# A hybrid layer kernel on one core: batch 0 prepared ahead of the turned weights, and one joint order for the setup and the first passes

## What is computed

```python
x = x + attention(_layernorm(x))    # w_qkv, b_qkv, w_out, b_out
x = x + ffn(_layernorm(x))          # router over 8 experts, top 2, and a shared expert
x = x + state_space(_layernorm(x))  # conv, scan over 512 tokens with 16 states
x = x + ffn(_layernorm(x))          # the same weights again
```

```python
q = jax.nn.elu(q) + 1
k = jax.nn.elu(k) + 1
rot_q = apply_rope(q)
rot_k = apply_rope(k)
attn_num = jnp.einsum('bhid,bhjd->bhij', rot_q, rot_k)
attn_denom = jnp.einsum('bhid,bhjd->bhij', q, k)
attn_weights = attn_num / attn_denom
```

## Time and profile before

| what | value |
|---|---|
| median of 3 runs | 3764.75 us (3763.28 to 3771.59) |
| profiled execution, its own time | 3763.91 us |
| its span, first to last instruction | 3761.8 us |
| PE busy | 3394.5 us (90%) |
| ACT busy | 3199.0 us (85%) |
| DVE busy | 2664.6 us (71%) |
| POOL busy | 1341.8 us (36%) |
| first score of pass 0 starts at | 73.94 us |
| `A.oT` of pass 0, 1 starts at | 168.25, 366.07 us |

### The profile page before, as it was taken

The page is one execution under the profiler, slowest core; times in us unless marked ns, Lnnn a source line. Parts: engine busy times, 40 slices in busy tenths (PEclk is TensorE's granted clock), DMA queues, the critical chain, the costliest instruction groups (busy, mean ns, idle before and its releaser), DMA issues. The chain is left out here.

```text
span 3761.8 us, 38380 instructions
## 1 busy us (share of the span) xinstructions
PE 3394.5 (90%) x11446; PEld 1446.9 (38%) x11446; DVE 2664.6 (71%) x3513; ACT 3199.0 (85%) x4034; POOL 1341.8 (36%) x758
## 2 busy tenths in 40 slices
PE   3896899999999999999999999999999999998847
PEld 1231334434343444434344443434344443434424
DVE  3537868687776868677686867778686877769582
ACT  2787899898999999899998989999998999886643
POOL 2112324344343434434342433424243443314251
PEclk9896899999999999999999999999999999999978
DMA  5324345455544545454454545454454645435332
GB/s 156 112 82 116 126 137 174 141 179 148 164 149 138 170 131 185 146 167 142 155 171 135 177 132 185 143 159 159 139 181 125 187 145 164 149 107 171 111 136 76
DMA packets 214847, 552.01 MB, mean 147 GB/s; under 512 B 25105, under 2 KB 96626, under 8 KB 214642
## 3 DMA queue, kind: packets, MB, share of 16 engines
q1 hardware_dynamic: 214642, 549.57, 47.4%
HBM read 488.65 MB, written 63.18 MB: 147 GB/s over the span
## 5 line engine op out<-in xcount | busy, mean ns | idle before, releaser
L785 PE MATMUL bank<-hF,wst 128*128 128x512 f32 x2304 | 1146.3, 619 | 29.7 <-ACT hF L887 15.2
L1332 POOL TENSOR_TENSOR yM<-yM,ws 128x1024 f32<-128x1024 f32 x240 | 630.6, 2628 | 1399.8 <-DVE ws L1231 1396.8
L1112 DVE TENSOR_TENSOR rPool<-bank,rPool 128x512 f32<-128x512 f32 x1024 | 700.5, 686 | 525.4 <-PE bank L713 411.5
L887 ACT ACTIVATE hF<-bank,cols 128x512 f32<-128x512 f32 x1152 | 771.6, 687 | 248.8 <-PE bank L774 233.6
L1025 ACT ACT_TABLE_LOAD x528 | 677.4, 1283 | 9.3
L887 ACT ACTIVATE rPool<-bank 128x512 f32<-128x512 f32 x1024 | 572.0, 597 | 92.5 <-PE bank L708 84.8
L772 PE MATMUL bank<-xnH,wst 128*128 128x512 f32 x1152 | 605.0, 525 | 30.3 <-ACT hF L887 18.3
L1224 DVE TENSOR_TENSOR_SCAN ws<-dAs,ws 128x1024 f32<-128x1024 f32 x256 | 598.7, 2345 | 7.2 <-ACT dAs L887 0.8
L785 PEld LDWEIGHTS bank<-hF,wst 128*128 128x128 f32 x2304 | 419.0, 193 | 464.2 <-issue 366.0
L713 PE MATMUL bank<-qpk,kpk 48*128 48x512 bf16 x1024 | 406.0, 398 | 97.8 <-DVE rPool L1112 93.6
L887 ACT ACTIVATE rPool<-rPool 128x2048 f32<-128x2048 f32 x256 | 490.5, 1916 | 2.1
(11 more groups left out here) (157 smaller groups left out, 2951.6 us busy)
## 6 DMA issues: line engine op xcount, KB each, us to landing
wst<-wscr SPq DMA_DIRECT2D x288, 768.0 KB, 5.9
bc<-bcscr SPq DMA_DIRECT2D x256, 512.0 KB, 4.6
cB<-gscr SPq DMA_DIRECT2D x256, 256.0 KB, 4.7
qscr<-parts SPq DMA_DIRECT2D x192, 128.0 KB, 2.4
kscr<-parts SPq DMA_DIRECT2D x192, 128.0 KB, 2.1
kpk<-kscr SPq DMA_DIRECT2D x128, 192.0 KB, 5.3
qpk<-qscr SPq DMA_DIRECT2D x128, 192.0 KB, 5.7
wscr<-wst SPq DMA_DIRECT2D x9, 512.0 KB, 5.5
```

The costliest lines, as they stand in the source:

```text
L785: pe.matmul(ps[FFN][:, :], w2, hF[:, (NCH * f + q) % HSLOTS, :], start=(c == 0), stop=(c == FC - 1)).then_inc(s_dn, 1)
L887: return nc.scalar.activation(out_, in_, fn, **kw)
L1112: v.tensor_tensor(rP[:, slot, c, :], ps[num_bank(b, s)][:, :], rP[:, slot, c, :], ALU.mult).then_inc(s_mul, 1)
L1332: g.tensor_tensor(yM[:, :, :], yM[:, :, :], ws[:, s % 3, :, :], ALU.add).then_inc(s_ya, 1)
```

## The change

**Setup.** Four of the 23 loads (w_qkv, its bias, and the two rotation tables) move to the front and count on a semaphore of their own, `s_wearly`; the other 19 still count on `s_wload`. The setup becomes items in the order tables (stage S): DVE's permutation waits only for the early four (`S.early`), PE turns the bias by itself (`S.bias`) between mean and variance of batch 0, and turns the other weights (`S.turn`) after the four projections, into three banks instead of six. Only the first `den` and the first `A.ln` wait for `s_setup`.

**Projections of batch 0.** The four `P.qk` go to four banks (4, 3, 5 and 7) and no longer wait for ACT. Rotation and subtractions (`P.rope`, `P.rest`) of batch 0 move from POOL to DVE. The six copies of each pack are issued half by SP and half by ACT (`P.pk` on ACT). The rest of the run's batches are as before.

**Order.** HEAD, FIRST, SECOND and pass 2 become one table START, whose words carry their pass, so that items of neighbouring passes can cross. Passes 14 to 17 become one table FINISH, and passes 3 to 13 still use MAIN. From the start of pass 3 to the end every engine has the same operations in the same order as before.

The diff, cut to its core (tables: two lines of many):

```diff
-HEAD = {
+START = {
...
     "SP": """
-    P.pk*4 P.ahead*2
+    -1:P.pk*4 0:W.store -1:P.ahead 0:P.in 0:W.store*2 -1:P.ahead 0:W.store*2 0:A.load 0:W.store*2 0:A.load 0:P.pk*4
...
-        N_WLOAD = 23
+        N_EARLY, N_WLOAD = 4, 19
+        QK_BANK = (PRE, 3, 5, 7)
...
-            head = numbered(HEAD[name], 0)
-            run(head, -1)
-            run(numbered(FIRST[name], 0), 0)
-            run(numbered(SECOND[name], 0), 1)
+            for i, stage, item, n in mixed(START[name]):
+                run([(stage, item, n)], i)
             main = numbered(MAIN[name], KEPT)
-            run(without(main, "H"), 2)
-            for i in range(3, NB - 1):
+            for i in range(3, NB - 2):
                 run(main, i)
-            run(without(main, "P"), NB - 1)
-            run(numbered(LAST[name], KEPT), NB)
-            run(numbered(END[name], NS), NB + 1)
+            for i, stage, item, n in mixed(FINISH[name]):
+                run([(stage, item, n)], i)
...
-            wl(rawqkv, w_qkv)
-            wl(brow, b_qkv.rearrange("(a n) -> a n", a=1))
+            for dst, src in ((rawqkv, w_qkv), (brow, b_qkv.rearrange("(a n) -> a n", a=1)),
+                             (ropeC[:, :], rope_cos), (ropeS[:, :], rope_sin)):
+                sp.dma_start(dst, src).then_inc(s_wearly, 16)
...
-                    for r in range(6):
+                    for r in range(3 if b == 0 else 6):
                         sp.dma_start(scratch[:, r, :], parts[:, u, ROWS_OF[n][r], :]).then_inc(s_pk[u], 16)
...
-                    pe.wait_ge(s_A_exp, floor(4 * b + n))
-                    pe.wait_ge(s_A_relu, floor(4 * b + n))
-                    pe.matmul(ps[PRE][:, :], wqk[:, n, :], xnA[:, :], start=True, stop=True).then_inc(s_A_qk, 1)
+                    if b == 0:
+                        pe.wait_ge(s_wqk, 1)
+                    else:
+                        pe.wait_ge(s_A_exp, floor(4 * b + n))
+                        pe.wait_ge(s_A_relu, floor(4 * b + n))
+                    bank = QK_BANK[n] if b == 0 else PRE
+                    pe.matmul(ps[bank][:, :], wqk[:, n, :], xnA[:, :], start=True, stop=True).then_inc(s_A_qk, 1)
...
+                elif name == "pk":
+                    t, u = divmod(n, 2)
+                    act.wait_ge(s_A_split, 4 * (n + 1))
+                    scratch = (qscr if t == 0 else kscr)[b, u].rearrange("g (d r) x -> (g d) r x", r=6)
+                    for r in range(3, 6):
+                        nc.scalar.dma_start(scratch[:, r, :], parts[:, u, ROWS_OF[t][r], :]).then_inc(s_pk[u], 16)
...
-            turn_in()
-            pe.wait_ge(s_setup, 1)
```

More of the change, by code:

```diff
@@ L50 @@
 """,
     "PE": """
-    P.load P.mean P.var P.qk*4
+    -1:P.load -1:P.mean -1:S.bias -1:P.var -1:P.qk*4 -1:S.turn 0:A.v 0:A.den*5 0:P.load 0:A.den*2 0:A.num 0:P.mean
+    0:A.den*2 0:A.num*2 0:A.den*2 0:A.num 0:A.av 0:P.var 0:A.num*4 0:A.den*3 0:P.qk 0:A.num*2 0:A.av 0:A.num
+    0:A.den*3 0:P.qk 0:A.den 0:A.num*2 0:A.av 0:A.den 0:P.qk 0:A.den*2 0:A.num*4 0:A.av 0:A.num 0:A.den*3 0:A.num
+    0:A.den 0:A.num 0:A.den 0:P.qk 0:A.num*2 0:A.den*2 0:A.num*2 0:A.av 0:A.den 0:A.num*2 0:A.den 0:A.av 0:A.den
@@ L56 @@
+    2:T.silu 2:M.silu*2 2:M.xp 2:M.silu 2:P.cast 2:M.silu 2:M.row 2:T.log 2:A.ln*2 2:M.dt 2:A.ex 2:A.ln 2:M.dt
+    2:A.ln 2:M.sp 2:T.gelu 2:G.gelu 2:T.log 2:M.decay 2:A.ln*2 2:A.ex 2:A.ln*3 2:M.decay 2:A.ln 2:M.decay 2:A.ex
+    2:T.gelu 2:G.gelu 2:P.cast 2:G.gelu*5 2:T.log 2:A.ln*4 2:A.ex 2:M.decay*2 2:T.gelu 2:G.gelu*2 2:P.cast
+    2:G.gelu*2 2:T.log 2:A.ln*4 2:A.ex 2:A.ln*4 2:A.ex 2:T.gelu 2:G.gelu*4 2:T.log 2:M.decay*2 2:A.oT
 """,
     "DVE": """
-    P.mean P.var P.til*4
+    -1:S.early -1:P.mean -1:S.bias -1:P.var -1:P.til*2 -1:P.rope -1:P.til*2 -1:P.rest*2 -1:S.take -1:P.rest
@@ L75 @@
-""",
-    "ACT": """
-    A.ln*6 A.ex A.ln P.load A.ln*2 A.ex P.mean P.var A.ln*3 A.ex P.qk A.ln*5 A.ex P.qk A.ln*3 A.ex P.qk A.ln*4 A.ex
-    A.ln*4 A.ex P.qk A.ln*4 A.ex A.ln*5 A.ex A.ln P.cast A.ln*4 A.ex A.ln*2 P.cast A.ex P.cast A.ln*3 P.cast A.ln*2
-    A.ex A.ln*3 P.cast A.ex P.cast A.ln*2 P.cast A.ln*3 P.cast A.ex A.ln*3 A.ex A.ln*4 A.ex A.oT
-""",
-    "DVE": """
-    A.v W.split*5 A.mul W.split A.mul*3 P.mean W.split A.mul*2 P.var A.mul*3 P.til A.mul*3 P.til A.mul*11 W.split
-    A.mul*9 W.split P.til*2 A.mul*32 A.close
@@ L223 @@
-""",
-    "DVE": """
-    E.mean E.var E.gate G.mean G.var G.router G.route G.part G.turn G.part*8
-""",
-    "POOL": """
-    G.add*8
+    14:H.add 14:N.acc*2 14:H.add*3 14:N.acc*5 14:F.add 14:P.rope 14:F.add 14:N.acc*2 14:P.rest 14:F.add*2
+    14:P.rest*2 14:P.rope 14:P.rest 14:F.add*3 14:M.take 14:P.rest*2 14:M.keep 14:M.acc 14:P.rest 14:G.add 14:P.rest
+    14:M.acc 14:G.add 14:M.acc*2 14:G.add*2 14:M.acc*2 14:P.keep 15:H.add 15:N.acc*2 15:H.add*3 15:N.acc*5
+    15:F.add*2 15:N.acc*2 15:F.add*5 15:M.take 15:M.keep 15:M.acc 15:G.add 15:M.acc 15:G.add 15:M.acc*2 15:G.add*2
@@ L249, in numbered, with mixed @@
             order.append((stage, name, count[part]))
+    return order
+def mixed(text):
+    start = dict(COUNT_FROM)
+    for name in ("bc", "decay", "dbx", "scan", "hc", "acc"):
+        start["N." + name] = KEPT
+    for name, n in G_AHEAD.items():
+        start["H." + name] = n
+    order, count = [], {}
+    for word in text.split():
+        head, _, times = word.partition("*")
+        i, _, part = head.partition(":")
+        stage, name = part.split(".")
+        for _ in range(int(times or 1)):
+            n = count.get(head, start.get(part, 0))
+            count[head] = n + 1
+            order.append((int(i), stage, name, n))
     return order
```

454 lines of the change are left out of this document (313 added, 141 removed).

## The result

The changed kernel takes 3749.56 us (median of 7 runs, 3743.20 to 3761.18) against 3764.75 us of the kernel before, timed beside it: a ratio of 0.9962, with an interval of 0.9946 to 0.9978. That is 14 us faster by the ratio, and 20 us above the forecast of 3730. So the two profiles are compared stage by stage and not by their sums.

What follows compares the result with a forecast made beforehand. Setup is bound by latency, passes from 3 on by their own work (PE 95% busy). 23 + 3 + 3 + 5 = 34 us off 3763.9 gives 3729.9, stated as 3730; own range 3720 to 3740, 8-in-10 range 3713 to 3747.

Steps and rivals of the forecast that it cites:

- the sum's 3 + 3 + 5 us for passes 0 to 2: Passes 0, 1 and 2: gains from order and fewer table loads, added to 23 us from the setup.
- Step 7: Setup, last pack: three issues per queue instead of six on one, landing at 44.1; one queue: first score 1.9 us later.
- step 6: Setup, DVE chain after the projections: 12.1 us plus five waits of 0.7 for ACT's casts, ending at 40.7.
- a bound of 4 us: Setup: unknown price of ACT's DMA issues, bounded at 2 us better and 4 worse.
- late early loads: Setup: the four early loads land with the rest, DVE starts at 13.4, some 7 us later: 3737; chance 0.08.
- the slower case: Pass 1: PE waits for batch 2's heads at its first score, delaying queued num; at 42 us, 3772; chance 0.03.
- the 3 us forecast: Pass 0: earlier first Exp and less ACT idling at the end, together 3.6 us, 3 taken; bounds 0 and 7.
- I took 3 us from 8.16 us of waiting: Pass 1: four fewer table loads and two products moved ahead of a scan product, 3 us; bounds -3 and 10.
- my bounds of 0 to 12: Pass 2: range around the 5 us gain from six removed table loads, 7.7 us.
- the 8 us that it would have added: Passes 1 and 2: with the skill's 1.38 us drain per table switch, time would be some 8 us lower.
- my test: Later passes: the prediction is wrong if they differ from the old ones by more than 2 us each.
- head-alone rival: Passes 0 to 2: crossing items changes nothing, only the setup's 23 us counts: 3741; chance 0.20.

Runs made afterwards that it cites:

- the twelfth kernel: The kernel before with the new setup, without pass 2's three empty table-load pairs, plus 31 unread matmuls ahead of the first score: 3751.60 us, ratio 0.9938.

## Why the prediction was wrong

The step that failed is the sum's 3 + 3 + 5 us for passes 0 to 2: the joint list with its ten saved table loads was to win 11 us there. The passes took 1.9 us more, 0.4 less and 2.1 more instead, 3.6 us more in all. The list alone, on the old setup, had ratios of 1.0031 and 1.0005, and the setup alone 0.9959, about as much as the whole change. The range was narrow too: a first score of 46 to 57 us with 3 to 20 us for the passes gives 3716 to 3744 by the prediction's own terms, not 3720 to 3740, and it held no case in which the passes lose. Here is each stage over all profiles of the two kernels, in us, from boundary to boundary:

| stage | before (2 profiles) | changed (3 profiles) | means differ | forecast |
|---|---|---|---|---|
| to the first score | 73.9, 74.6 | 52.4, 52.4, 52.2 | -21.9 | -23 |
| pass 0 | 95.0, 97.7 | 101.3, 95.8, 97.6 | +1.9 | -3 |
| pass 1 | 197.8, 195.8 | 197.3, 197.3, 194.6 | -0.4 | -3 |
| pass 2 | 215.9, 214.7 | 218.1, 215.9, 218.1 | +2.1 | -5 |
| passes 3 to 15 | 2821.1, 2828.5 | 2829.1, 2825.8, 2827.5 | +2.7 | 0 |
| the rest | 358.1, 358.8 | 361.2, 360.3, 359.8 | +2.0 | 0 |
| span | 3761.8, 3770.1 | 3759.4, 3747.5, 3749.8 | -13.7 | -34 |

**The setup was nearly right.** The early loads released DVE at 7.2 instead of 6.0; bias and variance ended at 14.4 instead of 13.4; the projections took 6.50 us and not 8.3, mostly because their eight matmuls, back to back, start 0.85 us apart from the second on, where I took half of a pair of 2.07 for each; the clock's record begins at 22.3 us, at 1.00, so a faster clock can have helped at their end alone. The chain on DVE ended at 41.47 (40.7 forecast), the last pack took 4.1 us from there and not 3.4, and the loads of the heads 6.6 and not 6.3. The second queue was priced wrong. Step 7's saving is there: from the last subtraction to the landing 4.09 us, against 5.74 with SP alone. But step 6 left ACT's issues out of the chain, or rather put them into a bound of 4 us, and they cost 1.39. The measured worth of the second queue is 0.26 us. The Trainium skill ("DMA: Bandwidth & Descriptors", Issuing engines are not separate DMA queues) says that a second issuer saves only the sequencer's time, usually small beside the DMA. Here that time was 1.65 us of 5.74, and most of it came back as casts that stand behind the issues. The rivals with late early loads, and the slower case, did not happen: PE never waits for the heads of batch 2 ahead of `A.close` of pass 1.

**Pass 0: the step took the joint list's gain and a clock that stays as it was.** Below, the time from the first score to the first product and then for each eight products (the last piece is seven), and in brackets how much of it was at the low clock, worked out from the starts of the products and the clock's records. The records of before begin only at 89.1 us; ahead of that its matmuls have the durations of the low clock (1.01 us for two), and it is counted as low; so is the start of pass 0 in the row of the joint order with the old setup, whose records begin at 90.4.

```
old order, old setup       8.8( 8.8) 12.6( 6.4) 13.8( 6.8)  9.6( 5.6) 11.1( 1.2) 10.9( 6.8)  8.2( 0.0)  9.7( 1.1)  7.9( 5.7)
old order, new setup       8.2( 8.2) 12.0( 5.1) 11.0( 0.0)  9.4( 3.4) 11.9( 3.5) 11.1( 9.3) 10.3(10.3) 10.9( 7.7)  8.5( 6.8)
joint order, old setup     8.3( 8.3) 14.3(10.9) 15.1(15.1) 12.3(12.3) 11.3( 3.0) 10.2( 8.2) 10.4(10.4)  9.8( 3.0)  7.9( 5.7)
changed kernel, first      6.5( 6.5) 14.7(11.3) 15.1(15.1) 12.3(12.3) 11.3( 3.3) 10.2( 7.9) 10.4(10.4)  9.8( 3.0)  8.0( 6.0)
changed kernel, second     6.5( 6.5) 14.9(11.5) 10.9( 1.0) 10.7( 6.9) 11.3( 3.3) 10.2( 7.9) 10.4(10.4)  9.8( 3.0)  8.0( 6.0)
changed kernel, third      6.5( 6.5) 14.9(11.5) 14.1(10.3) 10.2( 0.0)  9.7( 0.0) 10.2( 6.6) 10.4(10.4) 10.0( 3.5)  8.5( 6.8)
```

In these rows a stretch has nearly one length for one order and one amount of low clock, in different runs and from the eighth product on with either setup; the largest difference is 0.7 us (10.9 and 10.2 us with 6.8 low, in the two profiles of before). A microsecond at the low clock costs (15.1 - 10.9) / (15.1 - 1.0) = 0.3 us here. With the new setup the joint list does win 1.7 us up to the first product, and loses 2 to 3 in the next eight, where it had more low clock in every profile but that with a matmul ahead of each product (12.3 us with 2.6 low). Pass 0 took 95.4 us at best with it, 95.0 without: of the 3 us forecast, nothing stays. What went with the length of the pass, between 95 and 103 us over the 18 profiles, is the clock. The changed kernel had 76, 57 and 56 us of it in pass 0, before had 43 and 54, which at 0.3 us each is some 4 us. Whether the new setup draws more low clock, or three profiles happened to have it, is open; the experiments that filled the gap (58, 61 and 72 us of low clock with 31 matmuls) speak against the gap as the cause.

**Pass 1: ACT's waits are not a gain.** I took 3 us from 8.16 us of waiting ahead of `A.oT`. That wait is still there, and at the end of pass 0 the idle times of the earlier trace rows only moved: 5.67 and 2.78 us in place of 3.86 and 2.48. The ends of pass 1 and of pass 0, on ACT:

```profile
350.38 0.60 ACT L1040 ACTIVATE oT<-bank 128x512 f32<-128x512 f32 x1 [9.11 <-PE bank L888]
```
```profile
152.43 0.60 ACT L1040 ACTIVATE oT<-bank 128x512 f32<-128x512 f32 x1 [5.67 <-PE bank L888]
...
157.21 0.60 ACT L1040 ACTIVATE rPool<-bank 128x512 f32<-128x512 f32 x1 [2.78 <-PE bank L861]
```

ACT waits there for the last `av`, which itself waits for the last product of DVE. A faster or earlier ACT can't end that. Putting two pairs of loads back cost 0.1 us, so where they were put they are covered.

**Pass 2: the loads are near the path, and the list loses elsewhere.** Without the loads at the start of the pass, and otherwise in the old order, the pass takes 213.4, 212.3, 212.3 (joint order in pass 0 alone) and 215.0 us (the twelfth kernel), instead of 215.9, 214.7 and 215.9 (new setup alone). That is 2.2 us on the mean, within my bounds of 0 to 12. But the three short ones also have 23.9 us of low clock, the one of 215.0 has 30.7, and the three with the pairs 34.1, 30.7 and 34.1. With 30.7 us on both sides, the pass is 0.3 us longer without the pairs (215.0 against 214.7), or 0.4 shorter if products 24 to 32 are left out, where before's two profiles differ by 0.7 us as well. So most of the 2.2 us comes with the clock. Whether the removal drew it up or these profiles happened to have it is open: one and the same list shows both cases.

The step failed where it said that the joint list brings 5 us. The list has its first product 3.5 us earlier than before, gives most of it back in the next eight, and loses at the end (low clock in brackets):

```
to first product, then eight products each (low clock), and to A.close
before, first          9.9( 7.6) 31.3(21.0) 25.8( 2.2) 18.0( 0.0) 37.6( 0.0) 38.3( 0.0) 24.9( 3.4) 17.2( 0.0) 10.3( 0.0)  2.7( 0.0)
before, second         9.9( 7.5) 31.2(21.0) 25.8( 2.2) 18.0( 0.0) 36.9( 0.0) 38.3( 0.0) 24.5( 0.0) 17.1( 0.0) 10.3( 0.0)  2.7( 0.0)
changed kernel, first  6.4( 0.7) 33.9(26.6) 24.9( 0.0) 18.1( 0.0) 38.5( 0.0) 38.5( 0.0) 24.6( 0.0) 17.9( 0.0) 11.7( 3.4)  3.4( 0.0)
changed kernel, second 6.4( 0.6) 31.8(23.3) 24.9( 0.0) 18.1( 0.0) 38.5( 0.0) 38.5( 0.0) 24.6( 3.4) 17.9( 0.0) 11.8( 3.4)  3.4( 0.0)
old, no empty pairs    6.9( 0.0) 33.0(20.5) 24.2( 0.0) 18.0( 0.0) 36.9( 0.0) 38.3( 0.0) 24.8( 3.4) 17.1( 0.0) 10.3( 0.0)  2.7( 0.0)
the twelfth kernel     8.8( 6.5) 31.7(21.5) 25.9( 2.7) 18.0( 0.0) 37.6( 0.0) 38.3( 0.0) 24.5( 0.0) 17.1( 0.0) 10.3( 0.0)  2.7( 0.0)
```

At the high clock it takes 0.9 to 1.6 us more in products 24 to 32, some 0.8 in products 48 to 56 (in one profile the old order took 18.2 there too) and 0.7 at the end. The 1.4 us of the last seven products are the low clock: the joint list took 10.1 us there in two profiles without it. A microsecond at the low clock costs more here than in pass 0: by the two rows of the changed kernel (33.9 - 31.8) / (26.6 - 23.3) = 0.6 us. And in that list ACT is on the path at its end: with three pairs put back the pass takes 226.0. In the waits of pass 2, ACT waited for a matmul of F or G in before

```profile
ACT hF L887 <- PE bank L774: 10.9, 17, 1.3
```

and waits so in the changed kernel (us in total, times, longest):

```profile
ACT hF L1040 <- PE bank L927: 16.1, 21, 2.7
```

ACT is busy for 7.2 us less and the pass is 2.2 us longer, so it idles for 9.4 us more; 5.2 of them are here, and another 4.2 are one wait of the decay for DVE, which before's pass 2 does not have. What in the list costs the 0.9 to 1.6 us of products 24 to 32 was not taken apart.

A pair put back cost 2.6 us in the stretch with one pair and 5.9 in the one with two, with no idle time of ACT between load and Exp. That is the 2.57 us of the loads, and 0.4 us in each at most beside them; the stretch with two also had 3.4 us of low clock that it did not have before, which can be all of the 0.4. The Trainium skill ("ScalarE: Activation LUTs", What ACT_TABLE_LOAD costs) has a drain of some 1.38 us more for each; the trace does not agree, and the 8 us that it would have added were not there.

**The later passes** have the order of before and gained nothing, as forecast, but my test, that each lies within 2 us of before's, was a bad one. These passes go from 214.8 to 223.7 us; those without a low clock take 214.8 to 217.8, those with 10.2 us of it 219 to 224 (but for one pass 15, 216.8). The sums over passes 3 to 15 go from 2813.0 to 2834.1 over the 18 profiles, and before's two differ by 7.4. The rest after them is 2 us longer in the changed kernel. Over all kernels it takes 357.7 us with 90 us of low clock and 361.3 to 361.8 with 115 to 119, so most of it goes with the clock. But with 99.0 us it takes 358.1 in before, and 360.3 and 359.8 in the changed kernel. The joint order on the old setup, which has before's own tables here, takes 359.9 with 99.0, so the new table is not the reason; where in the stretch the low clock lies was not compared, and these 2 us stay open.

The head-alone rival (3741) was the nearest in kind: the joint list is worth nothing. It was right that nothing but the setup counts. Its number missed: the run with the head alone won 15 us, not 23. Its profile has a pass 0 of 101.7 us with 74.0 of low clock and the longest passes 3 to 15 of all, 2834.1, so the clock is the likely reason, but one profile does not show it for the median.

## What to carry to other kernels

Idle time of an engine at a boundary is a gain only when what ends it is what you move; ask who released it, and who released that one. An edit that reorders and removes at once should be split: here the removal alone went with 2.2 us less in pass 2, the removal and the new order together with 2.1 more. And time each stage in several profiles of the same kernel before a microsecond of it is explained, with the clock's share beside it: of the 2.2 us, most goes with less low clock.

## What the runs showed of the hardware

The granted clock of TensorE falls to 0.50 (1.2 GHz) without a long idle time of PE. With 31 matmuls in the gap PE was 98% busy until 52.1 us, idle for 1.23 us, busy for 1.29 of the next 2.00 us shown above, and the clock fell at 55.4; it stayed at 0.50 in stretches with PE busy for 92%. The fall comes at different moments in executions of one program that are alike up to then; from 67 us on the changed kernel had a low stretch of 34.1 us in one profile and of 3.4 in the next. In the total of one execution the records have 277 to 389 us of low clock, and executions of one kernel on one chip differ by up to 27 us (3745.67 to 3772.33 in the twelfth kernel).

A DMA issue costs ACT about as much as SP: 1.86 to 2.10 us for three, against 7.63 for twelve on SP. For a cast that stands behind it this is 1.4 us of delay.

The three runs of the changed kernel with matmuls in the gap have ratios of 0.9929, 0.9923 and 0.9933, the changed kernel 0.9962, 0.9946 and 0.9951. With the old order it is the other way: 0.9938 with the matmuls, 0.9928 and 0.9922 without. The profiles of the first three show no stage where this 0.2% would come from: pass 0 took 96.6, 95.4 and 100.0 us against 101.3, 95.8 and 97.6. It stays open.
